# Layer 2's gated layer in one stage

## The reference

```python
def _L2_ffn_ref(x, w12, w3, shared_w1, shared_w2, shared_w3, router_w, expert_bias):
    xf = x.reshape(-1, d)                                     # 1024 tokens of 256
    shared = jax.nn.silu(xf @ shared_w1.T) * (xf @ shared_w2.T) @ shared_w3.T   # hidden 1024
    scores = jax.nn.sigmoid(xf @ router_w.T)                  # 8 experts
    _, top_idx = jax.lax.top_k(scores + expert_bias, TOP_K)   # 2 per token
    mask = jax.nn.one_hot(top_idx, N_EXPERTS, dtype=xf.dtype).sum(axis=-2)
    gates = scores * mask
    h12 = jnp.einsum('td,ehd->teh', xf, w12)
    h1, h2 = jnp.split(h12, 2, axis=-1)                       # 256 each
    h = jax.nn.silu(h1) * h2 * gates[:, :, None]
    routed = jnp.einsum('teh,edh->td', h, w3)
    return (shared + routed).reshape(b, s, d)
```

## Time and profile before

| | us |
|---|---|
| median of 3 timed runs | 1550.95 (1546.78 to 1555.5) |
| the profiled execution | 1558.52 |
| its span, first to last instruction | 1556.7 |
| PE busy in the span | 1410.2 (91%) |
| DVE busy | 899.8 (58%) |
| ACT busy | 695.5 (45%) |
| POOL busy | 332.9 (21%) |

### The profile page before, as it was taken

The page is one execution under the profiler, slowest core; times in us unless marked ns, Lnnn a source line. Parts: engine busy times, 40 slices in busy tenths (PEclk is TensorE's granted clock), DMA queues, the critical chain, the costliest instruction groups (busy, mean ns, idle before and its releaser), DMA issues. The chain is left out here.

```text
span 1556.7 us, 24649 instructions
## 1 busy us (share of the span) xinstructions
PE 1410.2 (91%) x8362; PEld 1131.1 (73%) x8362; DVE 899.8 (58%) x1719; ACT 695.5 (45%) x1134; POOL 332.9 (21%) x348
## 2 busy tenths in 40 slices
PE   5799999799999999999998799999899786876994
PEld 4544444588888888888887777888678675765883
DVE  6778887655555555555556544444466455535556
ACT  5266667244344344344343265555443324443432
POOL 2101224212222222222221123333300033231100
PEclk8889999899999999999999799999999789897997
DMA  6811311111111111111100124555232115223000
GB/s 227 243 30 35 76 39 25 60 42 40 61 40 40 60 41 40 61 40 40 61 27 14 49 75 122 141 142 141 86 98 68 50 56 178 83 83 105 1 1 27
DMA packets 63703, 110.83 MB, mean 71 GB/s; under 512 B 10235, under 2 KB 39421, under 8 KB 62749
## 3 DMA queue, kind: packets, MB, share of 16 engines
q1 hardware_dynamic: 61773, 104.93, 23.1%
q0 software_dynamic: 1872, 5.13, 0.9%
HBM read 90.91 MB, written 18.97 MB: 71 GB/s over the span
## 5 line engine op out<-in xcount | busy, mean ns | idle before, releaser
L1217 DVE TENSOR_TENSOR hidden_l<-silu_l,up_l 128x512 f32<-128x512 f32 x128 | 88.1, 688 | 220.2 <-ACT silu_l L1157 220.2
L1157 ACT ACTIVATE silu_l<-gate_l 128x512 f32<-128x512 f32 x128 | 76.6, 599 | 308.6 <-PE up_l L75 308.6
L851 DVE TENSOR_REDUCE maxima<-a_scores 128x1 f32<-128x512 f32 x256 | 164.7, 685 | 41.0 <-PE a_scores L790 39.7
L73 PE MATMUL out_l<-dn_hi_l,h_hi_l 128*128 128x256 f32 x560 | 159.5, 285 | 5.4 <-DVE h_lo_l L2328 5.4
L818 ACT ACTIVATE probs<-b_scores 128x1024 f32<-128x1024 f32 x128 | 131.1, 1024 | 66.5 <-PE b_scores L747 64.5
L74 PE MATMUL out_l<-dn_lo_l,h_hi_l 128*128 128x256 f32 x560 | 159.1, 284 | 0.0
L75 PE MATMUL out_l<-dn_hi_l,h_lo_l 128*128 128x256 f32 x560 | 159.1, 284 | 0.0
L1189 POOL TENSOR_TENSOR gu_lo_l<-gu_raw_l,gu_hi_l 128x1024 fp32r<-128x1024 f32 x31 | 74.4, 2399 | 299.0 <-ACT gu_hi_l L1149 299.0
L73 PE MATMUL gate_l<-xnT_hi_n,gu_hi_l 128*128 128x512 f32 x280 | 112.6, 402 | 15.0 <-issue 11.8
L1241 DVE SCALAR_TENSOR_TENSOR x_sb<-out_l,cw,x_sb 128x256 f32<-128x256 f32 x256 | 109.0, 478 | 22.4 <-PE out_l L75 18.1
L73 PEld LDWEIGHTS out_l<-dn_hi_l,h_hi_l 128*128 128x128 f32 x560 | 108.4, 194 | 8.5 <-issue 5.9
(11 more groups left out here) (474 smaller groups left out, 3422.5 us busy)
## 6 DMA issues: line engine op xcount, KB each, us to landing
gu_raw_l<-w_units SPq DMA_DIRECT2D x32, 512.0 KB, 3.6
spread_l<-cw_rows SPq DMA_DIRECT2D x64, 256.0 KB, 3.9
dn_raw_l<-w_units SPq DMA_DIRECT2D x32, 256.0 KB, 2.7
k_stack<-k_stacks SPq DMA_DIRECT2D x8, 768.0 KB, 5.8
staged_l<-w_experts SPq DMA_DIRECT2D x24, 256.0 KB, 3.4
up_raw_l<-w SPq DMA_DIRECT2D x40, 128.5 KB, 3.5
dn_raw_l<-w SPq DMA_DIRECT2D x40, 128.0 KB, 2.1
phi_a<-fside SPq DMA_DIRECT2D x8, 512.0 KB, 3.3
```

Source lines behind the costliest of these rows:

```text
L73: pe.matmul(out, lhs[0], rhs[0], start=start, stop=False, skip_group_check=True)
L851: dve.tensor_reduce(maxima[k // 16][:, i // 2, i % 2:i % 2 + 1], a_scores[:, k % 2, :], X, ALU.max).then_inc(a_read, 1)
L1157: act.activation(silu[:, q % 2, :], gate[:, q % 2, :], ACT.Silu).then_inc(silu_done, 1)
L1217: dve.tensor_tensor(hidden[:, q % 2, :], silu[:, q % 2, :], up[:, q % 2, :], ALU.mult).then_inc(hidden_done, 1)
```

## The change

The three stages become two: `l2_sparse_phase`, with all eight shared units, routing, weight splits and the blocks, and `l2_return_phase`, which loads `routed` and adds it to x.

- `gu_raw` and `dn_raw` get two buffers (`DEPTH`); ACT splits gu two units ahead (after `high(n,1)`) and dn one unit ahead (after `high(n,0)`).
- Expert pieces: three before unit 0, then three per unit in units 0 to 6, two after the first half and one after the second. The low halves of the first 15 are made by POOL, of the other nine by DVE.
- Routing is cut into steps that stand in the halves of units 0 to 3 (`find_two`, `mark_two`, `read_ranks`, `find_starts`, `find_places`, `find_shares`, `find_experts`). Ranks are taken in unit 2. POOL sends four chunks in each of units 3 to 6 and sets the second row itself (`second_row`), after it has waited for the first eight sends.
- The blocks follow in the same stage, in banks and buffers of the units: the loaded slots lie in `staged`, the turned rows in `xnT_hi`, results and hidden values in `rows`. SP waits for all low halves and all sends before the first block's load. The shared result is added to x by DVE in its first four block steps (`add_shared`); `turn_h` and `block_down` of the first two blocks wait for that.
- `l2_return_phase` has eight loads of 256 KB (four pairs of chunks from each half of `routed`), a sum of the two, an addition to x, and the statistics, pair by pair.

```diff
-LATE2 = 2
+DEPTH = 2
...
+    def second_row(pool):
+        pool.wait_ge(r.sent[0], 16 * TC)
+        pool.wait_ge(r.rows_set, 2)
+        pool.tensor_tensor(rows[:, :, D:D + 1].rearrange("p c o -> p (c o)"), s.consts[:, TC:2 * TC], place[:, 1, :], ALU.subtract).then_inc(second_set, 1)
+        pool.tensor_copy(rows[:, :, D + 1:D + 2].rearrange("p c o -> p (c o)"), share[:, 1, :]).then_inc(second_set, 1)
+        pool.wait_ge(second_set, 2)
...
+def l2_sparse_phase(nc, g, d):
+    N, OUTS = NS2, 4
+    EARLY, EACH = 3, 3
+    BY_POOL = EARLY + EACH * 4
...
+        def pieces(n):
+            return range(EARLY + EACH * n, min(EARLY + EACH * (n + 1), PIECES))
...
+            def _(sp):
+                def load(n):
+                    if n >= DEPTH:
+                        sp.wait_ge(gu_lo_done, n - DEPTH + 1)
+                    sp.dma_start(gu_raw[n % DEPTH][:, :, :, :], d["w_shared2"][n, :, 0:2, :, :]).then_inc(gu_loaded[n % DEPTH], 16)
+                    if n >= DEPTH:
+                        sp.wait_ge(dn_lo_done, n - DEPTH + 1)
...
+                def stage(i):
+                    if i >= RING:
+                        done, count = lows_of(i - RING)
+                        sp.wait_ge(done, count)
...
+                for n in range(N):
+                    if n + DEPTH < N:
+                        load(n + DEPTH)
+                    for i in pieces(n):
+                        stage(i)
+                sp.wait_ge(we_lo_pool, BY_POOL)
+                sp.wait_ge(we_lo_dve, PIECES - BY_POOL)
+                for w in range(2):
+                    sp.wait_ge(route.sent[w], 16 * TC)
+                for b in range(BLOCKS):
+                    load_block(b)
...
+            def _(pe):
                 for n in range(N):
                     front(n, 0)
+                    if n == 2:
+                        pe.wait_ge(hidden_done, 4)
+                        route.take_ranks(pe)
                     if n >= 1:
                         down(n - 1, 1)
                     front(n, 1)
...
                     down(n, 0)
                 down(N - 1, 1)
+                pe.wait_ge(s.expert_set, 1)
+                pe.wait_ge(we_hi_done, PIECES)
+                pe.wait_ge(we_lo_pool, BY_POOL)
+                pe.wait_ge(we_lo_dve, PIECES - BY_POOL)
+                for step in range(NB2 + 3):
+                    if step < NB2:
+                        turn_x(step)
...
+            def _(act):
+                split_gu(1)
+                split_dn(1)
+                for i in range(EARLY):
+                    split_piece(i)
+                for n in range(N):
+                    mine = list(pieces(n))
+                    silu_of(n, 0)
+                    high(n, 0)
+                    if 1 <= n < N - 1:
+                        split_dn(n + 1)
+                    for i in mine[0:2]:
+                        split_piece(i)
+                    silu_of(n, 1)
+                    high(n, 1)
+                    if n == 0:
+                        route.sigmoid(act)
+                    if n + 2 < N:
+                        split_gu(n + 2)
+                    for i in mine[2:]:
+                        split_piece(i)
...
+            def _(pool):
+                low_gu(1)
+                low_dn(1)
+                for i in range(EARLY):
+                    low_piece(i)
+                for n in range(N):
+                    mine = [i for i in pieces(n) if i < BY_POOL]
+                    if 1 <= n < N - 1:
+                        low_dn(n + 1)
+                    for i in mine[0:2]:
+                        low_piece(i)
+                    if n + 2 < N:
+                        low_gu(n + 2)
+                    for i in mine[2:]:
+                        low_piece(i)
+                    if 3 <= n < 7:
+                        w, i = divmod(n - 3, 2)
+                        if n == 5:
+                            route.second_row(pool)
+                        route.send(pool, w, range(i * TC // 2, (i + 1) * TC // 2))
...
+            def _(dve):
+                for n in range(N):
+                    if n == 2:
+                        route.read_ranks(dve)
+                    product(n, 0)
+                    low(n, 0)
+                    if n == 1:
+                        route.mark_two(dve)
+                    if n == 2:
+                        route.find_starts(dve)
+                    if n == 3:
+                        route.find_shares(dve)
+                    mine = [i for i in pieces(n) if i >= BY_POOL]
+                    for i in mine[0:2]:
+                        low_piece(i)
+                    product(n, 1)
+                    low(n, 1)
+                    if n == 0:
+                        route.find_two(dve)
+                    if n == 2:
+                        route.find_places(dve)
+                    if n == 3:
+                        route.find_experts(dve)
+                    for i in mine[2:]:
+                        low_piece(i)
...
+                    if b < TC // 2:
+                        add_shared(b)
...
+def l2_return_phase(nc, g):
...
+                for i in range(PIECE):
+                    for w in range(2):
+                        a = w * T + 2 * i * P
+                        sp.dma_start(parts[w][:, 2 * i:2 * i + 2, :], g.routed[a:a + 2 * P, :].rearrange("(c p) e -> p c e", p=P)).then_inc(part_loaded[w][i], 16)
...
+                sum_parts(0)
+                for i in range(PIECE):
+                    add_parts(i)
+                    if i + 1 < PIECE:
+                        sum_parts(i + 1)
+                    dve.wait_ge(added, i + 1)
+                    take_stats(dve, g, (2 * i, 2 * i + 1))
...
-                l2_shared_phase(nc, g, d, "l2", 0, NS2 - LATE2)
-                l2_routed_phase(nc, g, d)
-            l2_shared_phase(nc, g, d, "l2b", NS2 - LATE2, LATE2)
+                l2_sparse_phase(nc, g, d)
+            l2_return_phase(nc, g)
```

More of the change, by code:

```diff
@@ L2115, in l2_shared_phase @@
+    r.find_two, r.mark_two, r.take_ranks, r.read_ranks, r.find_starts = find_two, mark_two, take_ranks, read_ranks, find_starts
+    r.find_places, r.find_shares, r.find_experts, r.second_row, r.send = find_places, find_shares, find_experts, second_row, send
+    return r
+def l2_sparse_phase(nc, g, d):
+    N, OUTS = NS2, 4
+    EARLY, EACH = 3, 3
+    BY_POOL = EARLY + EACH * 4
     with ExitStack() as ctx:
         def sb(name, shape, dt=F32):
-            return ctx.enter_context(nc.sbuf_tensor(f"{name}_{tag}", shape, dt))
@@ L2119, in two, with several @@
-        def two(name, shape, dt=F32):
-            return [sb(f"{name}{i}", shape, dt) for i in range(2)]
-        gu_raw, gu_hi, gu_lo = sb("gu_raw", [P, 2, KC, FS]), two("gu_hi", [P, 2, KC, FS], F32R), two("gu_lo", [P, 2, KC, FS], F32R)
-        dn_raw, dn_hi, dn_lo = sb("dn_raw", [P, D]), two("dn_hi", [P, D], F32R), two("dn_lo", [P, D], F32R)
+            return ctx.enter_context(nc.sbuf_tensor(f"{name}_l2", shape, dt))
+        def several(name, shape, dt=F32, n=DEPTH):
+            return [sb(f"{name}{i}", shape, dt) for i in range(n)]
@@ L2148, in pieces, with slot_halves @@
[L2148 to L2153 removed]
+        norm = normaliser(nc, ctx, g, "l2", out[:, :, :, :].rearrange("p (h k) j e -> p h k (j e)", h=2), rows[:, :, 0:D])
+        route = l2_dispatch(nc, ctx, g, d, out[:, 3, :, :].rearrange("p j e -> p (j e)"), up[:, 1, :], rows)
+        def slot_halves(t, i):
+            return [g.xnT_hi[:, i, :].rearrange("p (u k m) -> p u k m", u=4, k=KC)[:, t + j, :, :] for j in range(2)]
@@ new lines, in l2_sparse_phase @@
+        x_hi, x_lo, b_hi, b_lo = slot_halves(0, 0), slot_halves(2, 0), slot_halves(0, 1), slot_halves(2, 1)
+        slots = [staged[i][:, :, :].rearrange("p k f -> p (k f)")[:, 0:RW2] for i in range(BLOCKS)]
+        result = [rows[:, i, 0:D] for i in range(OUTS)]
+        b_silu, b_hidden = [rows[:, 4 + i, 0:D] for i in range(2)], [rows[:, 6 + i, 0:D] for i in range(2)]
+        banks = out[:, :, :, :].rearrange("p b j e -> p b (j e)")
+        x_bank, gu_bank = [gate[:, i, :] for i in range(2)], [up[:, i, :] for i in range(2)]
@@ L2181, in _ @@
[L2181 to L2191 removed]
+                for i in range(RING):
+                    stage(i)
@@ L2243, in _, with turn_x @@
                 down(N - 1, 1)
+                def turn_x(b):
+                    pe.wait_ge(s.block_loaded[b % BLOCKS], 16 * (b // BLOCKS + 1))
+                    if b >= 2:
+                        pe.wait_ge(x_hi_done, b - 1)
+                        pe.wait_ge(x_lo_done, b - 1)
+                    for k in range(KC):
+                        last = pe.transpose(x_bank[b % 2][:, k * P:(k + 1) * P], slots[b % BLOCKS][:, k * P:(k + 1) * P], g.ident[:, :])
+                    last.then_inc(x_turned, 1)
```

436 lines of the change are left out of this document (176 added, 260 removed).

## The result

| | kernel before | changed kernel |
|---|---|---|
| median of 4 timed runs, us | 1553.1 (1546.8 to 1555.5) | 1530.1 (1529.0 to 1530.8) |
| ratio, 95% interval | | 0.9852 (0.9832 to 0.9871) |
| span of the profiled execution, us | 1556.7 | 1527.0 |
| first gate product to layer 3's first load, us | 198.4 | 170.3 |
| layer 3's first load to the end, us | 126.6 | 131.3 |

A forecast was written before the change was run, and what follows sets the result against it. Layer 2's gated layer was seen as held by PE's weight waits, low clock, an idle gap and late units. Clean savings of 39.6 us less 5, 3, 1, 1.4 and 1 gave 28, hence 1523 us (own range 1517 to 1528; wider 1512 to 1534).

The forecast's parts named there:

- The sum: Layer 2's gated layer: 39.6 us saved if clean, less 5, 3, 1, 1.4 and 1, leaves 28 us.
- Units: Layer 2's shared units: eight take 79 us if nothing stalls, where six take 88.5.
- The port: Units 0 to 3: DVE's routing steps are held up by running POOL subtractions, costing 5 us, at most 7.8.
- The clock: Units: PE runs at a lower clock behind waits, costing 3 us within 0 to 9.
- From units to blocks: Between last unit and first block: PE's gap is 1 us, within 0 to 3, in place of 7.7.
- Blocks: The 23 blocks: 1 us less, from 2.4 gained by a warm start and up to 1 lost to DVE's additions.
- The return: After the blocks: eight loads replace the late units, 13 us in place of 32, saving 19.
- "Result, scatter, landing and barrier (1391.9 to 1398.1) stay": Between the last block and the return: this stretch keeps its length.
- "the same 28 us off it give 1523": Whole kernel: the 28 us saved come off the earlier timed median of 1551, giving 1523.
- The cause of the 11.8 us: Units: PE's four waits before gate products, 11.8 us, come from one gu_raw buffer and a late ACT split.
- The port decides: Rival, 24%: in units, every DVE-POOL meeting is lost, low clock comes three times, sends land late; 19 won, 1532.
- It doesn't do what it says: Rival, 3%: no barrier, but the first block waits as long for its slots; 7.7 stay, 22 saved, 1529.

The follow-up runs named there:

- small_pool: Changed kernel with GpSimd's 15 expert-piece subtractions cut to 8 of each 256 columns, leaving out part of the work: 1515.9 us, ratio 0.9749.
- barrier_back: Changed kernel with one barrier put back between the units and the blocks, nothing else moved: 1531.3 us, ratio 0.9849.
- early_l3: Changed kernel with layer 3's four weight loads issued in the return stage instead of at layer 3's start: 1526.2 us, ratio 0.9821.
- after_again: Changed kernel unedited, run again with a second profile: 1535.1 us, ratio 0.9879.
- best: Changed kernel with expert pieces split at other places, layer 3's weights loaded in the return stage, and idle products on TensorE: 1523.4 us, ratio 0.9801.
- both2: Changed kernel with expert pieces kept out of units 1 to 3 and layer 3's weights loaded in the return stage, no idle products: 1521.2 us, ratio 0.9791.
- one_raw: Changed kernel with one raw buffer each for gate/up and down, loaded and split only when the unit before is through: 1555.0 us, ratio 0.9998.

## Why the prediction was right, and where it was not

**The sum** came out: 28.1 us in the stage against 28, and 25.2 in the second pair of profiles. That the first lies within 0.1 is in part luck, as misses cancel: units 2.1 and the end 1.6 dearer than in the sum, the gap 1, the blocks 2.4 and the return 0.2 cheaper. Its terms:

- *Units*: 79 + 5 + 3 = 87 were forecast, 89.1 came. Cut free of meetings they take 80.3, near the 79. ACT, POOL, SP and the ring of three kept pace as worked out; all waits before gate products went.
- *The port*: 5 us within 0 to 7.8. PE's waits for h_lo before the last one are 1.24, 1.48, 0.45, 1.00 and 1.94, with 0.2 before the ranks 6.3. The value nearer to the upper end was right for the reason given: dn_lo and both pieces run just as the steps start (rows above).
- *The clock*: 3 us. One stretch, 4.1 us at 0.64, lost 4.1 x 0.36 = 1.5. Port and clock together were 8.8 by small_pool, 8 forecast.
- *From units to blocks*: 1 us within 0 to 3; 0 came, since the last send began at 1309.1, 5.3 before the block's first turn. The rule of the Trainium skill weighed there ("SBUF — State Buffer", Who interferes with whom) gave 0 as well. The trace doesn't contradict it, but no run here separates the causes of the longest send, 1.47 us.
- *Blocks*: mis-sized, 1 us forecast, 64.0 - 60.6 = 3.4 measured. The blocks began at 1.00 in place of 0.66, as the term hoped, but what that is worth was read too low: 9.86 us of work at 0.66 hold 9.86 x 0.34 = 3.4 us of lost clock, not 2.4. The loss of 1.4 that was set against it didn't come: PE is idle for 0.9 us of the first 10.6 (0.7 before) and for 0.1 of the rest (0.3 before), so DVE's four additions held up next to nothing.
- *The return*: 13 forecast, 12.8 measured.
- *"Result, scatter, landing and barrier (1391.9 to 1398.1) stay"* is a step that failed: 7.8 us in place of 6.2. 1.3 of the 1.6 is the longer way from the last scatter to the next load behind a stage with units and blocks in one, which barrier_back doesn't have.

**The step that failed most** is the last of the sum: "the same 28 us off it give 1523". It takes layer 3 as unchanged. It took 4.7 us more in the profile, and 4.8 in the second pair, so 28.1 became 23.4 and 25.2 became 20.3; the timed medians of the two sets lie 23.0 and 20.6 apart. A smaller part of the miss is the time that the 28 us were taken off: 1551.0 was the median of three runs, and with the fourth it is 1553.1. The parts of the 4.7, by offsets from layer 3's first load: the first weight product is 1.5 late (+7.9 against +6.4), as its weights take longer to land; that part is shown by early_l3, which brings it back and more. 0.8 more is lost from there to the first product of attention. 2.4 lies in attention, in products that run slow behind waits that are as long as before. The weights' landing, in the kernel before and in the changed one:

```profile
wqkvo_raw_f<-wqkvo SPq DMA_DIRECT2D x2, 512.0 KB, 4.6
```

```profile
wqkvo_raw_f<-wqkvo SPq DMA_DIRECT2D x2, 512.0 KB, 6.0
```

In after_again about the same 4.7 is made up otherwise: its scores, the first products of attention, start 3.2 late, counted from the transposes, and attention takes 1.5 more. One slow group of products with v, its first instruction in the timeline of the changed kernel and of the kernel before:

```profile
1499.36 0.55 PE L73 MATMUL attn_out_a<-v_hi_l,pT_hi_a 128*128 128x256 f32 x1 [2.46 <-DVE pT_lo_a L1912]
```

```profile
1530.44 0.36 PE L73 MATMUL attn_out_a<-v_hi_l,pT_hi_a 128*128 128x256 f32 x1 [2.46 <-DVE pT_lo_a L1912]
```

and the stretch of its 24 products in both, columns as in the earlier trace rows:

```profile
1499.30:1503.80 4.50, 4.44 (x24) 4.32 (x24) 0.16 (x1) 0.00 (x0) 0.00 (x0) 0.64 0.00 0
```

```profile
1530.40:1533.50 3.10, 3.06 (x24) 2.93 (x24) 0.16 (x1) 0.00 (x0) 0.00 (x0) 1.00 0.00 0
```

The same wait of 2.46 us ends at a mean clock of 0.64 (half, 1.2 GHz, and then full, 2.4 GHz) in the one and at 1.00 in the other: 1.4 us. Which of these waits ends slow differs from kernel to kernel. What decides it stays open; neither the return (small_pool has it, and no slow product) nor a cold start alone (best and both2 have slow ones behind an earlier start) settles it.

**The cause of the 11.8 us** was put as "one gu_raw buffer and a split that ACT reaches only after the unit before". one_raw's chain shows the second half of it; the buffer was not what was waited for there. The worth was underrated: in eight units with routing spread over them it is 23 us, as much as the whole change brings. With that part undone, and each unit at (112.1 - 17.2) / 7 = 13.6 us, the late units gone and the blocks without a gap leave the kernel at the time that it had before.

**The rivals**: By the number alone, 1530.1 lies nearer to two of them than to 1523. *The port decides* (1532) was wrong in the kind of its price: the stage won 25 to 28, not 19, and what was lacking was lost in layer 3. *It doesn't do what it says* (1529) falls with the missing gap; but its thought that the barrier was not the point is right, as barrier_back costs nothing in sum. "Perfetto Trace Analysis" of the Trainium skill (Optimizing Scalar/DVE Operations) says that moving work between GpSimd and VectorE might not help, as they share a read port. That they hold each other up agrees with the rows; but twelve subtractions moved from GpSimd to VectorE did help, 89.1 to 85.7 us of units, and nine of units 1 to 3 moved in time, three of them staying on GpSimd, helped more, to 81.0.

## What to carry to other kernels

Put work whose time is free (weight splits) where the other of two engines that hold each other up has only reductions or accumulator work, and look for the small operations on a path: a copy of 0.18 us alone cost 1.20 beside a 1.3 us subtraction. Count what stands behind a wait in an engine's order: a split that is ready early but ordered behind a late result is as late as the result. And carry the sum past the stage: the stages behind it start from other landings and another clock, here 4.7 us on 28.

## What the runs showed of the hardware

- In the rows here DVE is held to the end of a running POOL subtraction or not at all, by operation: copy of 128x8 1.20 us, two-input operation of 128x64 1.13, reduction of 128x64 0.22 at the same place, and the product of hidden with up, one operand in an accumulator bank, its usual 0.69 beside gu_lo (at 1256.51).
- It goes the other way too: POOL's dn_lo, 0.73 to 0.75 us otherwise, takes 0.88, 1.07, 0.87 and 1.26 where DVE's subtraction of h_lo was already running (since 1247.89, 1257.90, 1270.09 and 1303.56 in the changed kernel).
- A wait of 2.46 us of PE was followed by products at 0.64 in one kernel and at 1.00 in another, with the same program around it.
- From the last scatter's end to the next stage's first load it is 3.9 us behind a stage of blocks alone and 5.25 behind one of units and blocks, in every profile.
